# Spline attention: gated addition that accumulates a negated running minimum, gate in two pieces and clip in three

## The reference, cut to what matters

```python
sim = einsum('bhnd,bhdm->bhnm', q, k) / sqrt(dh)        # dh = 32, n = m = 3136
xs  = clip(nan_to_num(sim), -6, 6)
kan = base_w * silu(xs) + einsum('...k,k->...', b_splines(xs), coef)
attn = softmax(kan, axis=-1)
out = einsum('bhnm,bhmd->bhnd', attn, v)                # then Wo, and x + ...
```

## Time and profile before

| | us |
|---|---|
| median of 3 runs (lowest, highest) | 7373.56 (7359.88, 7383.81) |
| profiled execution: its time | 7378.02 |
| profiled execution: its span | 7376.0 |
| busy: TensorE / VectorE / ScalarE / GpSimd | 6612.3 / 6213.3 / 5765.7 / 5396.8 |

### The profile page before, as it was taken

How to read it: one execution, slowest core, us unless ns; L and a number is a source line. 1 busy time by engine, 2 the same in 40 slices (tenths; PEclk the granted TensorE clock), 3 DMA queues, 4 the chain that set the end, 5 groups by cost and what they waited for, 6 DMA issues and landing times. The chain is left out here.

```text
span 7376.0 us, 141185 instructions
## 1 busy us (share of the span) xinstructions
PE 6612.3 (90%) x40618; PEld 4490.3 (61%) x40618; DVE 6213.3 (84%) x9509; ACT 5765.7 (78%) x9040; POOL 5396.8 (73%) x3374
## 2 busy tenths in 40 slices
PE   6777889999699999999999999999999999999998
PEld 4655547677366666666666666666666666666666
DVE  4333665454499999999999999999999999999997
ACT  5445113333399999999999999999999999999997
POOL 4334000000299999999999999999999999999997
PEclk7888999999799999999999999999999999999998
DMA  2000000000200000000000000000000000000000
GB/s 73 21 19 26 1 0 0 0 0 0 63 11 1 1 1 1 1 1 11 1 1 1 1 1 1 11 19 1 1 1 1 1 2 2 4 4 4 4 4 6
DMA packets 75949, 56.14 MB, mean 8 GB/s; under 512 B 50776, under 2 KB 73464, under 8 KB 75032
## 3 DMA queue, kind: packets, MB, share of 16 engines
q1 hardware_dynamic: 72512, 53.88, 2.6%
q10 hardware_dynamic: 3288, 0.33, 0.0%
HBM read 37.80 MB, written 16.37 MB: 7 GB/s over the span
## 5 line engine op out<-in xcount | busy, mean ns | idle before, releaser
L1552 POOL TENSOR_TENSOR a_s<-a_s,a_v 128x784 f32<-128x784 f32 x1568 | 2912.6, 1858 | 306.1 <-ACT a_s L1763 287.6
L1588 PE MATMUL a_right_sides<-a_s,diag_d 128*128 128x392 f32 x6272 | 2284.5, 507 | 8.4 <-POOL a_s L1552 1.0
L1588 PEld LDWEIGHTS a_right_sides<-a_s,diag_d 128*128 128x128 f32 x6272 | 1132.1, 190 | 1052.4 <-POOL a_s L1552 309.3
L1684 DVE SCALAR_TENSOR_TENSOR a_kan<-a_s,spline_c,a_kan 128x784 f32<-128x784 f32 x1568 | 1621.4, 1034 | 50.7 <-issue 0.3
L1611 PEld LDWEIGHTS a_weighed<-a_V,a_probT 112*128 112x128 f32 x10976 | 1375.5, 193 | 162.2
L1545 POOL TENSOR_TENSOR a_inner<-a_inner,a_x 128x784 f32<-128x784 f32 x784 | 1459.0, 1861 | 0.0
L1611 PE MATMUL a_weighed<-a_V,a_probT 112*128 112x65 f32 x10976 | 1366.3, 270 | 0.0
L1763 ACT ACTIVATE a_s<-a_v 128x784 f32<-128x784 f32 x1568 | 1335.3, 852 | 4.6
L1754 ACT ACTIVATE a_v<-a_a 128x784 f32<-128x784 f32 x1568 | 1336.0, 852 | 0.3
L1600 PE MATMUL a_turned<-ident,a_prob 128*112 128x128 f32 x5488 | 856.6, 278 | 229.8 <-ACT a_probT L1770 228.5
L1655 DVE TENSOR_SCALAR a_x<-a_scores 128x392 f32<-128x392 f32 x1568 | 874.6, 558 | 19.9 <-PE a_scores L1575 19.9
(11 more groups left out here) (196 smaller groups left out, 5814.3 us busy)
## 6 DMA issues: line engine op xcount, KB each, us to landing
rows<-bias_rows_dram SPq DMA_DIRECT2D x112, 91.0 KB
X<-in_x_dram SPq DMA_DIRECT2D x4, 1568.0 KB, 13.5
a_q<-q_dram SPq DMA_DIRECT2D x392, 16.0 KB, 2.0
mask<-in_window_mask_dram SPq DMA_DIRECT2D x56, 98.0 KB
v_dram<-V SPq DMA_DIRECT2D x14, 227.5 KB, 2.3
a_V<-v_dram SPq DMA_DIRECT2D x4, 796.2 KB, 8.8
q_dram<-Q SPq DMA_DIRECT2D x14, 224.0 KB, 1.9
k_dram<-K SPq DMA_DIRECT2D x14, 224.0 KB, 1.9
```

The costliest lines, as they stand in the source:

```text
L1552: eng.tensor_tensor(s, s, v, ALU.mult).then_inc(cubed, 1)
L1588: mm = eng.matmul(up[:, j, 0:SUB], steps[i][:, :], cubes[g][:, SUB * j:SUB * (j + 1)], start=(i == 0), stop=(i == 1))
L1684: eng.scalar_tensor_tensor(F, banked((s1, s2)[j][g][:, :]), c[:, 3 + j:4 + j], F, ALU.mult, ALU.add).then_inc(left_added, 1)
```

## The change

- `clip` is three instructions for each quarter: bank 0 whole (392 columns), then bank 1 in two pieces of 196; the semaphore `clipped` still counts 2 for each quarter, at the first and at the last piece.
- `gate` is two instructions, one for each bank, and stands at the start of quarter g of the list for quarter g-3 (before: at the end of the quarter ahead, for the same data). `right_gated` counts 2 for each quarter.
- `add_right` computes -(kan + gated) with scale=-1.0 and accumulates a minimum that starts from the minimum of the quarter before it (`gmin[:, g-1]`, a value read from SBUF); `gmin[:, 3]` is minus the row's maximum. The exponential takes scale=-1.0 and that bias. `row_max` and `negated_max` are gone, and the wait for `exp_done` moves to `add_right` of g = 3.
- VectorE's list is new: `gate` bank 0, (`invert` in g = 1, `add_output` in g = 2), `add_tanh`, `gate` bank 1, `times_x`, `clip` 0, `left` 0, `clip` 1, `left` 1, `clip` 2, `add_right`.

```diff
-                def gate(g):
+                def gate(g, j):
...
-                        eng.scalar_tensor_tensor(banked(part(r, g)), banked(x[g][:, :]), 0.0, U, ALU.is_gt, ALU.mult).then_inc(right_gated, 1)
+                        eng.scalar_tensor_tensor(part(r, g)[:, at], x[g][:, at], 0.0, up[:, j, 0:SUB], ALU.is_gt, ALU.mult).then_inc(right_gated, 1)
...
-                        eng.tensor_scalar(x[g][:, SUB * j:SUB * (j + 1)], scp[:, j, 0:SUB], 6.0, -6.0, ALU.min, ALU.max).then_inc(clipped, 1)
+                        first, end = ((0, SUB), (SUB, SUB + SUB // 2), (SUB + SUB // 2, 2 * SUB))[j]
+                        bank = first // SUB
+                        ins = eng.tensor_scalar(x[g][:, first:end], scp[:, bank, first - SUB * bank:end - SUB * bank], 6.0, -6.0, ALU.min, ALU.max)
+                        if j != 1:
+                            ins.then_inc(clipped, 1)
...
-                        eng.wait_ge(right_gated, n + 2)
+                        eng.wait_ge(right_gated, 2 * n + 4)
                         eng.wait_ge(left_added, 2 * n + 10)
+                        if g == 3:
+                            eng.wait_ge(exp_done, 4 * t + 4)
+                        eng.wait_ge(all_added, n + 1)
...
-                        eng.tensor_tensor_reduce(out=f, in0=F, in1=f, scale=1.0, scalar=-3.0e38, op0=ALU.add, op1=ALU.max,
-                                                 accum_out=gmax[r][:, g:g + 1]).then_inc(all_added, 1)
+                        eng.tensor_tensor_reduce(out=f, in0=F, in1=f, scale=-1.0, scalar=gmin[r][:, g - 1:g] if g else 3.0e38, op0=ALU.add, op1=ALU.min,
+                                                 accum_out=gmin[r][:, g:g + 1]).then_inc(all_added, 1)
...
                 for g in range(4):
-                    (g2, l2), (g3, l3) = (((g - back) % 4, int(g < back)) for back in (2, 3))
-                    between = {1: ([(invert, 3)], []), 2: ([], [(add_output, 4)]), 3: ([(row_max, 1)], [(negated_max, 1)])}.get(g, ([], []))
-                    order += [(add_tanh(g3), l3)] + between[0] + [(times_x(g3), l3)] + between[1] + [(left(g3, 0), l3), (clip(g, 0), 0), (left(g3, 1), l3),
-                              (clip(g, 1), 0), (add_right(g3), l3), (gate(g2), l2)]
+                    g3, l3 = (g - 3) % 4, int(g < 3)
+                    small = {1: [(invert, 3)], 2: [(add_output, 4)]}.get(g, [])
+                    order += [(gate(g3, 0), l3)] + small + [(add_tanh(g3), l3), (gate(g3, 1), l3), (times_x(g3), l3), (clip(g, 0), 0), (left(g3, 0), l3),
+                              (clip(g, 1), 0), (left(g3, 1), l3), (clip(g, 2), 0), (add_right(g3), l3)]
...
-                        eng.wait_ge(max_ready, t + 1)
-                        eng.activation(part(r, g), part(r, g), ACT.Exp, bias=nmax[r][:, :]).then_inc(exp_done, 1)
+                        eng.wait_ge(all_added, 4 * t + 5)
+                        eng.activation(part(r, g), part(r, g), ACT.Exp, scale=-1.0, bias=gmin[r][:, 3:4]).then_inc(exp_done, 1)
```

More of the change, by code:

```diff
@@ L1460, in kan_attention3 @@
         inner = [sb(f"inner{g}", [P, QUART]) for g in range(2)]
-        gmax = [sb(f"gmax{r}", [P, 4]) for r in range(2)]
-        rmax = [sb(f"rmax{r}", [P, 1]) for r in range(2)]
-        nmax = [sb(f"nmax{r}", [P, 1]) for r in range(2)]
+        gmin = [sb(f"gmin{r}", [P, 4]) for r in range(2)]
         rinv = sb("rinv", [P, 1])
@@ L1478, in kan_attention3 @@
         (loaded, q_ready, inverted, heads_folded, o_ready, y_made, x_added, out_stored, margin_set, s_made, clipped, v_ready, s_ready, cubed, line_made, inner_made, tanh_made, with_tanh, based, left_added,
-         right_made, right_gated, all_added, max_found, max_ready, exp_done, turned, copied, weighed, placed, waits_met_v, waits_met_p) = (
+         right_made, right_gated, all_added, exp_done, turned, copied, weighed, placed, waits_met_v, waits_met_p) = (
             sem(n) for n in ("loaded", "q_ready", "inverted", "heads_folded", "o_ready", "y_made", "x_added", "out_stored", "margin_set", "s_made", "clipped", "v_ready", "s_ready", "cubed", "line_made", "inner_made",
-                             "tanh_made", "with_tanh", "based", "left_added", "right_made", "right_gated", "all_added", "max_found",
-                             "max_ready", "exp_done", "turned", "copied", "weighed", "placed", "waits_met_v", "waits_met_p"))
+                             "tanh_made", "with_tanh", "based", "left_added", "right_made", "right_gated", "all_added",
+                             "exp_done", "turned", "copied", "weighed", "placed", "waits_met_v", "waits_met_p"))
         with nc.Block() as block:
@@ L1581, in stage @@
                         n = 4 * t + g
-                        eng.wait_ge(right_gated, n + 1)
+                        eng.wait_ge(right_gated, 2 * n + 2)
                         if g == 0:
@@ L1617, in project_out @@
                     eng.wait_ge(x_added, t + 4)
-                    eng.wait_ge(right_gated, 4 * t + 16 if not isinstance(t, int) else min(4 * t + 16, 4 * BLOCKS3 + 1))
+                    eng.wait_ge(right_gated, 8 * t + 32 if not isinstance(t, int) else min(8 * t + 32, 8 * BLOCKS3 + 2))
                     rows = slice(VW * (p % 2), VW * (p % 2 + 1))
@@ L1643, in _ @@
             def _(dve):
-                def gate(g):
+                def gate(g, j):
                     def stage(eng, t, r, p):
+                        at = slice(SUB * j, SUB * (j + 1))
                         eng.wait_ge(right_made, 4 * t + g + 5)
                         eng.wait_ge(turned, 7 * t + min(2 * g + 2, 7))
-                        eng.scalar_tensor_tensor(banked(part(r, g)), banked(x[g][:, :]), 0.0, U, ALU.is_gt, ALU.mult).then_inc(right_gated, 1)
+                        eng.scalar_tensor_tensor(part(r, g)[:, at], x[g][:, at], 0.0, up[:, j, 0:SUB], ALU.is_gt, ALU.mult).then_inc(right_gated, 1)
                     return stage
@@ L1705, in invert @@
                     eng.reciprocal(rinv[:, :], op[:, VW:V1]).then_inc(inverted, 1)
[L1707 to L1714, removed]
                 dve.sem_inc(clipped, 2)
@@ L1718, in _ @@
                 dve.sem_inc(left_added, 8)
-                dve.sem_inc(right_gated, 1)
+                dve.sem_inc(right_gated, 2)
                 dve.sem_inc(all_added, 1)
```

## The result

The changed kernel takes 7482.09 us (median of 4 runs, 7476.98 to 7487.87), the kernel before 7368.3 us in the runs beside it: ratio 1.0151, 95% interval 1.0138 to 1.0163. It is slower. The ratio makes it 111 us, where 108 were forecast (added to the profiled execution of the kernel before); the forecast time was 7480 us.

A forecast was written before the change was run, and what follows sets the result against it. VectorE was taken as the bound at 27.31 us a block. Four clip-to-clip distances summed to 27.89, taken as +0.55 over 196 blocks: +108 us on 7378.0, 7486, less 4.5 for the median, 7480; range 7390 to 7540.

The forecast's parts named there:

- What bounded the kernel before: Spline attention: VectorE, 98.8% busy and waiting for no other engine, is the bound; a block takes 27.31 us.
- The loop through tanh, copy, turn and scores: Clip 0 to the next clip 0 through three engines: formerly at most 6.14 us, now sets the pace of three quarters.
- its three steps: Clip 0 to clip 0: g = 1 to 2 7.08 us, 2 to 3 mean 6.99, 3 to 0 mean 6.83.
- invert ahead of add_tanh: g = 0 to 1: invert waits for the last weigh steps, so clip 1 comes 6.99 us after clip 0.
- VectorE's own work: VectorE without waits for scores: 6.64 us a quarter, 26.83 a block for 27.31.
- The start value from SBUF: add_right's minimum read from SBUF: 0 to 0.01 us with 0 taken, bounds -0.01 and +0.07.
- the new waits: add_right's waits for the accumulator read and for exponentials two blocks back: 0 to 0.03 us.
- VectorE stays the bound: Rival: clip 0 never waits for scores, block 26.83 us or 27.1 with invert's wait, 7280 to 7330; chance 0.12.
- Stalls: VectorE's waits at clip 0 and invert: 1.06 us a block.
- Interleaving gives nothing: Rival: VectorE's dependent pairs cost no more than independent ones, 28.06 us a block, 7520; chance 0.11 shared with dearer pieces.
- Short pieces cost more: Rival: each 196-column clip takes 0.42 us, up to +0.48 a block, 7575; chance 0.11 shared with no interleaving gain.
- TensorE's clock stays at 1.00: TensorE: busy share falls to about 90% from 92% in the window, granted clock stays at 1.00.

The follow-up runs named there:

- Experiment 9: Kernel before with only TensorE's order changed, scores(2), scores(3) and scores(0) ahead of the turns; ratio 0.9996.
- experiment 2: Changed kernel with TensorE's scores(2), scores(3) and scores(0) ahead of turn(2), turn(4) and turn(6); ratio to the kernel before 1.0061, 7417.14 us.
- experiment 3: Changed kernel with the clip of bank 1 whole again, between the two lefts; ratio to the kernel before 1.0245, 7552.4 us.
- Experiment 1: Changed kernel with invert behind the second half of the gate instead of the first; ratio to the kernel before 1.0139.
- experiment 10: Changed kernel with each quarter's minimum starting from a constant and one reduction over the four minima; ratio to the kernel before 1.0131.
- experiment 7: Changed kernel with gate in three, clip in two, invert behind the second gate piece, constant start value and one reduction; ratio to the kernel before 0.9896, 7296.78 us.
- experiment 11: Changed kernel with scores ahead of the turns, invert behind the second half of the gate, constant start value and one reduction; ratio to the kernel before 0.9979.
- experiment 6: Changed kernel with gate in three, clip in two, and invert behind the second gate piece; ratio to the kernel before 0.9894, 7299.42 us.
- 8: The kernel of experiment 7 with scores ahead of the turns on TensorE; ratio to the kernel before 0.9881, 7291.7 us.
- 4: Kernel before with only the reduction changed: negated sum, minimum starting from the previous one in SBUF, no row_max or negated_max; ratio 1.0095.
- experiment 5: Changed kernel with the roles swapped, gate in three pieces and clip in two; ratio to the kernel before 1.0167.

## Why the prediction was right

*What bounded the kernel before*, and that it had no wait to lose: right. Experiment 9 left VectorE with the same work and changed nothing.

*The loop through tanh, copy, turn and scores*: right in place and size. Of its three steps two are within 0.01 us and the third within 0.06 of the forecast. Experiments 2 and 9 show the cause by taking it away at a point that is not in the change.

*invert ahead of add_tanh*: right in kind, forecast 6.99, measured 7.10. In the changed kernel:
```profile
4024.42 0.57 DVE L1656 TENSOR_SCALAR a_x<-a_scores 128x392 f32<-128x392 f32 x1
...
4027.02 1.90 PE L1609 MATMUL a_weighed<-a_V,a_probT 112*128 112x65 f32 x16
...
4028.95 0.17 DVE L1711 RECIPROCAL a_rinv<-a_weighed 128x1 f32<-128x1 f32 x1
4029.15 1.04 DVE L1669 SCALAR_TENSOR_TENSOR a_kan<-a_scores,half_base,a_inner 128x784 f32<-128x784 f32 x1
```
The reciprocal starts 4.53 behind clip 0, where 4.55 was forecast (the rows of the prediction give 4.50; the 0.05 behind the end of the weigh steps it added without saying so). What was missed is the step behind it: add_tanh follows 0.20 later, not 0.07. In experiment 3, which has the same order but no wait at invert, it follows after 0.08; so a small instruction that had to wait delays the next by more than its distance in a full queue. Experiment 1 shows what the early invert cost: 0.29 in its own quarter, of which 0.15 can't be had back as long as ScalarE sets the pace of the next.

*VectorE's own work*: too low. The half gate (0.47), the quarter clip (0.35 long, 0.27 apart), add_output (0.20) are as worked out. Two terms were not. The start value from SBUF was taken at nothing and costs 0.06 three times a block; the bound of 0.07 held it, and the row chosen for the value, a 128-column instruction, did not bear on this one. And from the second left to add_right, with a clip between them, it takes 1.26 where 1.22 was worked out. The start value isn't why, since add_right of g = 0 starts from a constant and follows as late (4019.43 to 4020.68 in VectorE's timeline, 1.25). In experiment 10, where add_right also has no wait for the accumulator read before it, it is 1.23 (6411.47 to 6412.70); so most of it goes with the new waits, which the prediction had at 0 to 0.03 and left out of its sum. A quarter is then 6.67 without a start value from SBUF (g = 3 to 0 in experiment 2), and VectorE's block 4 x 6.67 + 0.18 + 0.20 + 0.07 = 27.13 without waits, for 26.83. The rival "VectorE stays the bound" was therefore priced 60 us too well at its low end: it would hardly have gained.

*Why the time came out nonetheless*: a quarter whose pace the loop sets doesn't see VectorE's extra work (experiment 10). Stalls are 0.5 at the clips and 0.3 at invert, 0.8 where 1.06 were worked out, and the work is 0.30 more; together they are the same. Part of the close hit is luck: 27.89 was rounded down to 27.86 (+0.55), the windows show 27.94, and the beginning of the pipeline took the rest back.

*Interleaving gives nothing*: wrong, as weighed. A quarter with clips that don't wait is 6.67, 6.73 with the start value (experiment 2), and 6.61 at best in experiment 7, for 6.83; the sentence of the Trainium skill ("VectorE: DVE Perf Modes", The DRAIN you can't avoid) on semaphores that cost nothing (the advice to minimize the count of instructions stands in the same page's Rules for kernel authors) doesn't hold for these 784-column instructions: add_tanh lets a half gate start after 0.95 (4008.07 to 4009.02), and times_x, which waits for it, after 1.07. The interleave is a gain if its pieces are the gate's. With the clip's it was a loss, but not because of the pieces as such: with scores ahead of the turns, invert late and a constant start (experiment 11), undisturbed blocks with the same pieces are the shortest of all, 26.90.

*Short pieces cost more*: out. The 196-column clip takes 0.35, not 0.42.

*TensorE's clock stays at 1.00*: right for the changed kernel (no slow stretch in its trace between the filling of the pipeline and its end), but thin: five of its neighbours had 15 to 72.

*A reading of the rows*: the gate and add_right give way 0.07 before their end, not 0.08 to 0.09 (0.96 long, 0.89 apart); the sum uses the distances, so nothing hangs on it.

## What to carry to other kernels

A tile that two engines use in turn makes a loop; write down its length before splitting or spreading any step on it, because time between the first and the last piece is added to the loop even where the engine is no busier. Fill the gaps of dependent instructions with pieces of a stage that has slack in its own loop (here the gate), not with those of the tightest one (the clip): with invert late in both, 1.1% faster (experiment 6) against 1.4% slower (experiment 1). Move small steps as late as their reader allows: one reciprocal in the wrong place, with what followed on TensorE, was worth 2.7%.

## What the hardware did that was not expected

- Neighbours on VectorE, start to start, for a first instruction of 1.03 to 1.04: 0.95 if the next is independent; if it waits for the first, 1.07 (add_tanh, times_x), 1.14 (times_x, left), 1.25 (left, add_right in experiment 3, where add_right also waits for the accumulator read before it). The margin differs by pair.
- A reciprocal that had to wait for TensorE was followed by the next instruction after 0.20 us (the changed kernel), one that had not after 0.08 (experiment 3).
- A start value from SBUF lengthens the 784-column add-and-reduce from 0.96 to 1.02 us.
- TensorE's granted clock can fall to its lower level (1.2 GHz) for some microseconds in a stage where it is otherwise about 90% busy, at fairly regular intervals. Once the pipeline had filled, there were none in the changed kernel and in experiments 6, 7, 8 and 10, one in 9, five in 4, and 15 to 72 in 1, 2, 3, 5 and 11, at 1.0 to 2.8 us each. The longest idle time of TensorE just ahead of them was 0.9 us (experiment 5) to 1.35 us (2). What brings it on was not settled, and the length of one idle time isn't enough: in experiment 9 TensorE idles for 1.25 us ahead of fold_heads in every block, and one slow stretch followed; in experiment 2 for 1.3 to 1.35, and 15 followed; experiments 6 and 7 have idle time of 0.9 to 1.1 in nearly every block and none, experiment 5 has 0.9 and 39.
